# Adding the lower neighbours of a diffusion step inside the transfer

## The reference

```
def L0(y, zX, zY, zR):                 # diffusion
    lap_x = left + right - 2 y         # neighbours along a row, reflected at the edges
    lap_y = above + below - 2 y        # neighbouring rows, reflected at the edges
    return zX * lap_x + zY * lap_y + zR * y * (1 - y)
x = x + L0(x)
x = x + pooled(x)      # tanh(x W1 + b1) v, masked softmax over 1024 rows, sum of rows
x = x + linear(x)      # 512x512 weight, chosen by a token of the batch
x = x + adapter(x)     # 512 -> 128 -> 512, relu, then the layer norm of the sum
```

## Time and profile before

| | |
|---|---|
| median of 3 runs | 703.36 us (699.14 to 703.6) |
| the profiled execution | 703.28 us |
| its span, first to last instruction | 701.6 us |
| PE busy | 572.5 us (82%) |
| DVE busy | 537.7 us (77%) |
| POOL busy | 358.2 us (51%) |
| ACT busy | 324.1 us (46%) |
| share of the transfer engines' span: queue of SP, of POOL, of ACT | 28.4%, 17.2%, 6.3% |
| moved in all | 99.40 MB |

### The profile page before, as it was taken

One profiled execution on the slowest core, in us unless ns is written; L12 is line 12 of the kernel. 1 busy time (PEld: TensorE's weight loads), 2 busy tenths in 40 slices (PEclk: granted clock), 3 DMA queues, 4 the chain that ended last, 5 costly groups with the idle time before them and its releaser, 6 DMA issues.

```text
span 701.6 us, 10274 instructions
## 1 busy us (share of the span) xinstructions
PE 572.5 (82%) x2928; PEld 457.0 (65%) x2928; DVE 537.7 (77%) x1149; ACT 324.1 (46%) x545; POOL 358.2 (51%) x263
## 2 busy tenths in 40 slices
PE   0247768979799788879889798898899798999992
PEld 0125646768668676668758676577768686688771
DVE  4565768699968998599968998498977899567422
ACT  1253445344745456235555266244564357543431
POOL 7242662348617565257636566075653678127232
PEclk9998889999999999899999999998999899999996
DMA  5471047325693187514693277622785166334364
GB/s 196 156 242 68 0 167 225 120 60 118 230 284 63 39 247 193 184 45 90 221 275 109 39 203 198 214 60 47 238 226 178 30 151 222 77 76 92 75 128 83
DMA packets 62838, 99.40 MB, mean 142 GB/s; under 512 B 11040, under 2 KB 15648, under 8 KB 62800
## 3 DMA queue, kind: packets, MB, share of 16 engines
q1 hardware_dynamic: 44240, 65.42, 28.4%
q0 software_dynamic: 9344, 16.79, 17.2%
q10 hardware_dynamic: 9216, 16.78, 6.3%
HBM read 65.42 MB, written 33.55 MB: 141 GB/s over the span
## 4 chain that ended last, share of the span: by engine, by line
PE 30%; DVE 28%; issue 17%; POOL 16%; ACT 3%; DMA 1%; SPq 1%; POOLq 0%; DVEq 0%; ACTq 0%
PE y L540 9%; POOL x2l L473 7%; PE front_ps L638 5%; PE front_ps L563 5%; POOL xu L430 5%; DVE mask L1031 3%; DVE x2f L1185 3%; PE front_ps L586 3%; POOL xd L438 2%; DVE xd L1052 2%; DVE xu L1044 2%; DVE mask L1035 2%; DVE pn L1139 2%; PE front_ps L571 2%; DVE x L1059 2%
## 5 line engine op out<-in xcount | busy, mean ns | idle before, releaser
L473 POOL TENSOR_TENSOR x2l<-x2f,x2h 128x1024 fp32r<-128x1024 f32 x32 | 89.8, 2813 | 55.5 <-DVE x2f L1185 44.1
L455 POOL TENSOR_TENSOR norm<-norm 128x1 f32<-128x1 f32 x64 | 44.4, 702 | 143.1 <-DVE norm L1209 142.8
L540 PE MATMUL y<-wth,x2h 128*128 128x512 f32 x256 | 103.8, 406 | 11.0 <-DVE wtl L1151 11.0
L430 POOL TENSOR_TENSOR xu<-xu,xd 128x1024 f32<-128x1024 f32 x32 | 79.5, 2485 | 62.7 <-DMA xd<-in_x 61.6
L540 PE MATMUL y<-wtl,x2h 128*128 128x512 f32 x256 | 103.1, 403 | 0.0
L540 PE MATMUL y<-wth,x2l 128*128 128x512 f32 x256 | 102.6, 401 | 0.0
L638 PE MATMUL front_ps<-th_pt,x 128*128 128x129 f32 x512 | 76.7, 308 | 28.7 <-DVE x2f L1185 28.5
L638 PEld LDWEIGHTS front_ps<-th_pt,x 128*128 128x128 f32 x512 | 74.0, 221 | 33.6 <-DVE x2f L1185 30.8
L438 POOL TENSOR_TENSOR xd<-xn 128x1024 f32<-128x1024 f32 x32 | 66.6, 2080 | 34.0 <-ACT xn L758 30.5
L552 PE MATMUL front_ps<-ident,x 128*128 128x128 f32 x256 | 35.5, 290 | 50.3 <-DVE x L1059 50.3
L778 ACT ACTIVATE xd<-xn,cur 128x1024 f32<-128x1024 f32 x32 | 39.8, 1243 | 77.6 <-DVE xu L1044 77.6
(11 more groups left out here) (120 smaller groups left out, 1185.8 us busy)
## 6 DMA issues: line engine op xcount, KB each, us to landing
xn<-in_x SPq DMA_DIRECT2D x32, 512.0 KB
out<-x ACTq DMA_DIRECT2D x64, 256.0 KB, 2.0
out<-o_sb POOLq DMA_DIRECT2D x64, 256.0 KB, 4.4
xd<-in_x SPq DMA_DIRECT2D x24, 512.0 KB
xu<-in_x SPq DMA_DIRECT2D x24, 512.0 KB
wn<-in_L_cond_weight SPq DMA_DIRECT2D x8, 1024.0 KB, 5.5
xu<-in_x SPq DMA_DIRECT2D x8, 256.0 KB
xd<-in_x SPq DMA_DIRECT2D x8, 256.0 KB
```

The lines of the kernel that those rows point to most:

```text
L430: pool.tensor_tensor(xu[:, sl, :, :], xu[:, sl, :, :], xd[:, sl, :, :], ALU.add).then_inc(pool_b, 1)
L473: pool.tensor_tensor(x2l[q][:, k, :], x2f[:, k % 2, :], x2h[q][:, k, :].bitcast(F32), ALU.subtract).then_inc(x2l_ready, 1)
L540: ins = mm(dst, lhs, rhs, start=first and q == 0, stop=last and q == len(parts) - 1, skip_group_check=True)
```

## The change

`load_x` no longer loads `xd`. The rows below come by transfers that POOL issues with `accum_op=ALU.add`, straight from `x` in HBM onto `xu`. They are issued by `add_below`, which takes the place of `above_and_below` and waits for the same loads. The count of loads for each chunk falls from 6, 3, 3, 6 to 5, 2, 2, 2. `add_below` issues one transfer of 512 KB for chunks 0 to 2 and four for chunk 3 (256, 224, 30 and 2 KB). `scale_rows` waits for these transfers. `left_and_right` no longer waits for `pool_b`, as `xd` is only written there now.

```diff
-        X_DMAS = [6] + [3] * (NC - 2) + [6]
+        X_DMAS = [5] + [2] * (NC - 1)
+        BELOW_DMAS = [1] * (NC - 1) + [4]
...
-                    get(xd[:, sl, :, :], r0 + 1, r0 + 1 + size)
...
-            def above_and_below(m, c):
-
-                sl = c % 2
+            def add_below(m, c):
+
+                sl, r0, size = c % 2, c * 2 * P, 2 * P
                 pool.wait_ge(x_loaded[sl], x_count(m, c))
-                pool.tensor_tensor(xu[:, sl, :, :], xu[:, sl, :, :], xd[:, sl, :, :],
-                                   ALU.add).then_inc(pool_b, 1)
+
+                def add(dst, lo, hi):
+                    src = x[bass.ds(m, 1), lo:hi, :]
...
+                    pool.dma_start(dst, src, accum_op=ALU.add).then_inc(below_added[sl], 16)
+
+                if c == NC - 1:
+                    add(xu[:, sl, 0, :], r0 + 1, r0 + 1 + P)
+                    add(xu[0:112, sl, 1, :], r0 + P + 1, r0 + P + 113)
+                    add(xu[112:P - 1, sl, 1, :], r0 + P + 113, S)
+                    add(xu[P - 1:P, sl, 1, :], S - 2, S - 1)
+                else:
+                    add(xu[:, sl, :, :], r0 + 1, r0 + 1 + size)
 
             def left_and_right(m, c):
 
                 sl = c % 2
                 pool.wait_ge(halo, NC * m + c + 1)
-                pool.wait_ge(pool_b, NC * m + c + 1)
...
                 act.wait_ge(cur_ready, m + 1)
-                act.wait_ge(pool_b, NC * m + c + 1)
+                act.wait_ge(below_added[sl], below_count(m, c))
```

More of the change, by code:

```diff
@@ L194, in build @@
         pool_a = sem("pool_a")
-        pool_b = sem("pool_b")
+        below_added = [sem("below_added0"), sem("below_added1")]
         scaled_rows = sem("scaled_rows")
@@ L258, in build, with below_count @@
         CONST_DMAS, CONST_MADE = 7, 3
-        X_DMAS = [6] + [3] * (NC - 2) + [6]
+        X_DMAS = [5] + [2] * (NC - 1)
+        BELOW_DMAS = [1] * (NC - 1) + [4]
         def x_count(n, c):
             return n * 16 * sum(X_DMAS[c % 2::2]) + 16 * sum(X_DMAS[c % 2:c + 1:2])
+        def below_count(n, c):
+            return n * 16 * sum(BELOW_DMAS[c % 2::2]) + 16 * sum(BELOW_DMAS[c % 2:c + 1:2])
         def before(t, ring):
@@ L424, in constants @@
                 pool.memset(minus_half[:, :], -0.5).then_inc(const_made, 1)
-            def above_and_below(m, c):
-                sl = c % 2
+            def add_below(m, c):
+                sl, r0, size = c % 2, c * 2 * P, 2 * P
                 pool.wait_ge(x_loaded[sl], x_count(m, c))
-                pool.tensor_tensor(xu[:, sl, :, :], xu[:, sl, :, :], xd[:, sl, :, :],
-                                   ALU.add).then_inc(pool_b, 1)
+                def add(dst, lo, hi):
+                    src = x[bass.ds(m, 1), lo:hi, :]
+                    if hi - lo == size:
+                        src = src.rearrange("b (j p) d -> p (b j) d", p=P)
+                    else:
+                        src = src.rearrange("b p d -> p (b d)")
+                    pool.dma_start(dst, src, accum_op=ALU.add).then_inc(below_added[sl], 16)
[4 more added lines that the diff above has]
+                    add(xu[P - 1:P, sl, 1, :], S - 2, S - 1)
+                else:
+                    add(xu[:, sl, :, :], r0 + 1, r0 + 1 + size)
             def left_and_right(m, c):
@@ L484, in program @@
                 if m is not None:
-                    above_and_below(m, 0)
+                    add_below(m, 0)
                     left_and_right(m, 0)
@@ L489, in program @@
                 if m is not None:
-                    above_and_below(m, 1)
+                    add_below(m, 1)
                     left_and_right(m, 1)
@@ L508, in program @@
                 if m is not None:
-                    above_and_below(m, 2)
+                    add_below(m, 2)
                     left_and_right(m, 2)
@@ L514, in program @@
                 if m is not None:
-                    above_and_below(m, 3)
+                    add_below(m, 3)
                     left_and_right(m, 3)
```

## The result

| | before | after |
|---|---|---|
| median of 15 runs | 701.82 us (699.14 to 704.5) | 708.8 us (705.67 to 714.39) |
| ratio, 95% interval | | 1.010 (1.0078 to 1.0122) |
| span of the profiled execution | 701.6 us | 705.6 us |
| PE / DVE / POOL busy | 572.5 / 537.7 / 358.2 us | 573.8 / 483.5 / 335.4 us |
| mean clock granted to PE | 0.949 | 0.939 |

The kernel became 1.0% slower, about 7 us, where I had forecast 12.8 us less.

What follows compares the result with a forecast made beforehand. PE was taken as busiest (82%), waiting for `x2f` because POOL's additions hold DVE's masks. Sum: 6 x (-3.9 + 2.3) - 3.2 = -12.8 us from 703.28, so 691 us; range 681 to 714, leaving out 2 in 10.

Steps and rivals of the forecast that it cites:

- late term: Chunk 3's additions land after ACT needs them and PE waits: +2.3 us for each of six batches.
- It lands 3.8 to 4.4 us later: Chunk 3's last transfer, issued at 265.3, lands about 269.5; landings after 267.2 delay PE, giving +2.3 us a batch.
- early term: DVE's masks freed from POOL's addition of chunk 1, so PE's wait for `x2f` shrinks: -3.9 us for each of six batches.
- I let it wait for an issue too: First mask operation L1031 on DVE assumed held until `finish`'s issue ends at 306.93, then running to 307.25.
- PE has adapter and linear products to do: Chunk 0's addition holds up DVE's L1134 for 2.31 us, but PE has other work: counted nothing, at most 2.1 us.
- DVE must wait for chunk 3 anyway, so nothing: Chunk 2's addition would be some 1 us late for DVE, counted as no cost.
- rival 2: Chunk 3's additions land late beside the next batch's weights: loss 5.5 us a batch, 710 us; chance 0.23 with or without rival 1.
- the bound of +5.5 us a batch: Upper bound for chunk 3: its additions take the 9.7 us stores had in this stretch, landing at 272.7.
- a gain of 3.2 us together: Batches m = 0 and 1: `times_x` and `diffuse` of chunk 2 no longer slowed beside POOL, 1.6 us each.
- Rival 1: DVE's masks still held up by POOL's issues: gain 1.1 in place of 3.9 us, 707 us at worst; chance 0.22 alone.
- Rival 3: Chunk 3's additions land before 267.2, hidden, and the early gain stays whole: -26.6 us, 677 us; chance 0.13.

## Why the prediction was wrong

The sum failed on both sides. Its late term, 6 x 2.3 us, is where the sign was lost: the step "It lands 3.8 to 4.4 us later" and the nothing for chunk 2 give a loss of 13.8 us, and the runs show 53. Its early term, 6 x 3.9 us, gives a gain of 23.4, and the runs show 47. The 708.8 us lie inside the stated range of 681 to 714 only because the two errors are opposite, which is luck.

**The early part: the mechanism right, the term mis-sized.** The prediction put six times 3.9 us, 23.4, for chunk 1. The kernel with chunk 1 alone gained 37.4. Half of the 14 us missing is the clock.

- *The masks did not wait for an issue.* The step "I let it wait for an issue too" failed: L1041 took 0.32 us during L472's issue. `add_around` 0 starts 4.7 us earlier where nothing else is late, not 3.9; over the six batches it is 4.1, so this adds little to the term. The half microsecond at 306.18 in which L1031 "did not run" cannot be laid to the issue: with only the order changed, L1031 took 0.32 us beside the same issue. What held it there before L430 is recorded as running stays open. The Trainium skill, "SBUF — State Buffer", section "Who interferes with whom", says that a VectorE operation in a mode that takes both port pairs and a GpSimd instruction block each other fully, and that writing descriptors needs a port too. For POOL's additions the traces agree (2835 ns against 324). For the issue they hardly do: a store's issue did not hold L1041. At most the end of an issue of 256 rows did a little: in the first batch of the kernels for chunks 0 and 1 and for chunk 1 the mask operation began beside one and took 0.43 and 0.51 us.
- *The slow clock behind the wait.* The earlier trace rows had 3.73 us for sixteen matmuls of L638 behind the wait of 4.23 us, against 2.49 us in the changed kernel, and the window of 228 to 236 us has a granted clock of 0.84. I read the 4.23 us as all there was to gain there. PE's busy time fell by 7.2 us in the kernel with chunk 1 alone (572.5 to 565.3) and by 12.7 us in the kernel with chunks 0 and 1. With the 24.3 us by which PE's wait for `x2f` fell in the kernel with chunk 1 alone (28.5 to 4.2) and 4.4 us of waits for `x` (50.3 to 45.9) that makes 35.9 of the 37.5 us by which its span is shorter.

**Chunk 0: the cover did not hold.** "PE has adapter and linear products to do" was the reason for nothing, with a bound of 2.1 us a batch. It measured 9.4 us, three quarters of that bound over six batches, and more than half of the difference is again PE's busy time.

**Chunk 2: "DVE must wait for chunk 3 anyway, so nothing."** The step looked at who waits for chunk 2, not at whom it delays. I let the addition delay chunk 3's loads by part of 1.0 us and had them land earlier than before (263.0 against 264.01). They take 7.2 to 7.8 us from issue to landing in the first three batches of the changed kernel, where my landing at 263.0 meant about 5.9. With chunk 3 added in the old way, a third of the cost is in the first batch, where chunk 2's addition is not hidden and takes 9.6 us. Measured: +13 to +15 us.

**Chunk 3: rival 2's mechanism, with its own upper bound.** "It lands 3.8 to 4.4 us later" took the landings of stores in quiet stretches, though the earlier trace rows had 9.7 us from this very stretch and the earlier trace rows 219 GB/s beside it. It lands 9.2 to 10.0 us after the first issue. I had it as the bound of +5.5 us a batch; chunk 3 cost 36 to 40 us in eight batches. That the four additions take about what the stores took there is partly chance: these are other transfers, onto another memory. Two more things are in there: PE's slow clock behind the new wait (0.9 us on the transposes and 0.8 us on the score products), and the batches m = 0 and 1, where I had expected a gain of 3.2 us together from the shorter `times_x` and `diffuse`. They lost 0.4 and 4.1 us (table of marks).

**The rivals.** Rival 1 fell: the masks run beside the issues. Rival 2 happened in its mechanism, but not with its sum: its 710 us, near to the 708.8 measured, come from -3.9 and +5.5 us a batch, and the real terms are larger on both sides, -47 and +53 us in all. Near a cancellation the forecast's error is that of the terms and not of the difference, and these two errors, 24 us early (47 against 23.4) and 42 us late (53 against 13.8 - 3.2), stand against a range 33 us wide. Rival 3's rule speaks of bytes alone. The Trainium skill, "DMA: Bandwidth & Descriptors", section "Anatomy of one DMA — SWDGE (gpsimd) path", gives an estimate of 3.2 us for 512 KB. Measured are 4.0 us for plain copies, 5.8 us for adding ones, and 9.2 to 10.0 us for the four beside the weights.

**What makes the landing late** is settled in part. The weights account for some 2.4 us of it (9.7 on average against 7.3), the adding together with its longer issue for about 1.3 us at unchanged weights (8.4), the four transfers for about 0.6 us once the weights are gone and for little beside them. Whether the weights harm by their bytes or by their many small packets, I did not separate. Nor did I move the transfer to another place in the batch.

**A version that beats both kernels** came out of it: the transfer for chunks 0 and 1 alone, 656.0 us, 6.8% below the kernel before. There the landing has slack (of the seven batches from m = 1 on, ACT waits for it in one, 2.4 us), and POOL's additions are gone from beside the masks. Around chunk 3, from 260 to 282 us, POOL was busy for 12.5 of 22 us and the transfer engines for 79%: POOL had time for its additions, and the engines had little.

## What to carry to other kernels

Moving work from an engine to the transfer engines is judged place by place: what the engine is in the way of there, how full the transfer engines are there, and what they carry behind the new transfer. Price a wait of PE with the clock that it costs behind it, and for a landing take the row from the same stretch rather than a quiet one. Where gain and loss are both several times their difference, a version that keeps only the gaining half is worth more than a better estimate of the sum; here it was 47 us against a difference of 7.

## What the runs showed of the hardware

- An adding transfer from HBM into SBUF occupies the transfer engines longer: 137 to 212 GB/s with the engines busy, against 389 to 423 GB/s for plain loads in the same row. 16.8 MB occupy the 16 engines for 104 us when adding, and for 52 us without. 512 KB land in 5.8 us (median) against 4.0 us.
- Adding also slows what runs beside it: 1 MB of weights takes 7.3 us, and 5.6 us beside the same transfers without adding.
- The mask operation on DVE runs at full speed beside POOL's issue of a store: 0.32 us, where it waits for the end of a POOL addition (2.8 us on average). Beside the end of an issue of 256 rows it took 0.43 and 0.51 us in two kernels.
- POOL's issue of an adding transfer of 256 rows takes 1.24 us (I had worked out 1.3), and 1.54 us right behind another issue. The four issues for chunk 3 take 3.48 us (2.8). Without adding it is 0.80 and 2.3 us.
- After PE has waited 6.9 us its granted clock is 0.71 from 278 to 285 us, and eight transposes take 1.94 us instead of 1.04.
